# A fused macaron block on one core: the first packed chunk from SBUF to SBUF on two queues, and the expert weights fetched later

## The reference

```
x = x + 0.5 * ffn(layernorm(x))
x = x + dilated_attention(layernorm(x))
x = x + 0.5 * ffn(layernorm(x))

ffn(x):  x = conv3(x) + conv_b                   # 128 -> 128 channels, 3 taps
         q, k, v = split(x @ wqkv.T + bqkv)      # 16 heads of 8
         ctx = softmax(q k^T / sqrt(8)) v        # 512 x 512 for each head
         x = layernorm(x + ctx @ wo.T + bo) * g1 + b1
         probs = softmax(x @ gate_w + gate_b)    # 8 experts, all of them used
         y_e = relu(x @ w1[e] + b1[e]) @ w2[e] + b2[e]        # 128 -> 512 -> 128
         return layernorm(x + sum_e probs[e] * y_e) * g2 + b2
```

## Time and profile before

| | |
|---|---|
| median of 3 runs | 1558.36 us |
| profiled execution | 1559.22 us |
| its span, first to last instruction | 1557.5 us |
| mean granted PE clock | 0.982 |
| busy: PE, DVE, ACT, POOL | 96%, 75%, 72%, 65% |
| DMA, mean rate | 84 GB/s |

### The profile page before, as it was taken

The page is one execution under the profiler, slowest core; times in us unless marked ns, Lnnn a source line. Parts: engine busy times, 40 slices in busy tenths (PEclk is TensorE's granted clock), DMA queues, the critical chain, the costliest instruction groups (busy, mean ns, idle before and its releaser), DMA issues.

```text
span 1557.5 us, 26116 instructions
## 1 busy us (share of the span) xinstructions
PE 1502.6 (96%) x8318; PEld 832.5 (53%) x8318; DVE 1160.8 (75%) x1834; ACT 1121.3 (72%) x1636; POOL 1014.9 (65%) x978
## 2 busy tenths in 40 slices
PE   4888999999999999999999999999999999999997
PEld 3433555555555555555555555555555555555476
DVE  3767677878778787777877778777777777767486
ACT  2466777677776777777677777777777777777776
POOL 3521668767686776868767686776757677667343
PEclk7799999999999999999999999999999999999999
DMA  7433333152332514233142331514323251521111
GB/s 177 119 92 86 96 87 85 49 140 53 81 91 56 130 42 105 74 88 91 49 131 61 81 92 45 141 48 116 83 75 98 69 117 43 142 51 36 41 43 33
DMA packets 75309, 130.06 MB, mean 84 GB/s; under 512 B 10613, under 2 KB 39206, under 8 KB 70566
## 3 DMA queue, kind: packets, MB, share of 16 engines
q1 hardware_dynamic: 73894, 124.19, 31.2%
q0 software_dynamic: 1280, 4.20, 1.0%
HBM read 97.42 MB, written 29.62 MB: 82 GB/s over the span
## 4 chain that ended last, share of the span: by engine, by line
PE 84%; DVE 8%; issue 3%; SPq 1%; DMA 1%; ACT 1%; POOL 1%; DVEq 0%; ACTq 0%; POOLq 0%
PE hid_y L1013 16%; PE ctx_ps L1208 14%; PE hid_y L1017 13%; PE hid_y L1014 13%; PE score L1056 12%; DVE negmax L881 3%; PE misc L1013 2%; PE score L1076 1%; PE misc L1148 1%; DVE x1n L349 1%; PE score L1013 1%; PE misc L1105 1%; PE misc L1164 1%; PE misc L1141 1%; PE misc L1014 1%
## 5 line engine op out<-in xcount | busy, mean ns | idle before, releaser
L881 DVE TENSOR_REDUCE negmax<-score 128x2 f32<-128x1024 f32 x484 | 590.5, 1220 | 239.4 <-PE score L1056 239.4
L592 POOL TENSOR_TENSOR hidl<-hid,hidh 128x512 fp32r<-128x512 f32 x456 | 584.4, 1293 | 258.1 <-DVE hidh L838 140.8
L711 ACT ACTIVATE probs<-score 128x1024 f32<-128x1024 f32 x468 | 479.5, 1024 | 108.7 <-PE score L1076 108.5
L740 ACT ACTIVATE hid<-hid_y,cols 128x512 f32<-128x512 f32 x484 | 330.9, 684 | 161.9 <-PE hid_y L1017 154.2
L1208 PE MATMUL ctx_ps<-probs,V 128*18 128x512 f32 x2048 | 271.5, 602 | 3.2 <-DVE ctxT L888 3.2
L1056 PE MATMUL score<-Kp,Qp 24*128 24x512 f32 x968 | 244.9, 500 | 23.8 <-DMA Kp<-k_parts_dram 16.1
L1076 PE MATMUL score<-Qp,Kp 32*128 32x512 f32 (+1 forms) x1024 | 265.9, 499 | 0.0
L1013 PE MATMUL hid_y<-x1h,w1h 128*128 128x512 f32 x484 | 236.2, 488 | 1.5 <-DVE negmax L881 1.3
L369 POOL TENSOR_TENSOR yacc<-yacc,gated 128x512 f32<-128x512 f32 x127 | 170.6, 1343 | 61.8 <-DVE gated L854 61.8
L737 ACT ACTIVATE hidh<-hid_y,cols 128x512 fp32r<-128x512 f32 x256 | 174.7, 682 | 34.4 <-PE hid_y L1017 31.9
L1056 PEld LDWEIGHTS score<-Kp,Qp 24*128 24x128 f32 x968 | 90.5, 183 | 197.4 <-issue 138.2
(11 more groups left out here) (203 smaller groups left out, 1828.4 us busy)
## 6 DMA issues: line engine op xcount, KB each, us to landing
gate_b<-gate_dram SPq DMA_DIRECT2D x128, 256.0 KB, 3.6
q_parts_dram<-q_parts SPq DMA_DIRECT2D x48, 256.0 KB, 3.0
k_parts_dram<-k_parts SPq DMA_DIRECT2D x48, 256.0 KB, 3.1
Qp<-q_parts_dram SPq DMA_DIRECT2D x64, 192.0 KB
Kp<-k_parts_dram SPq DMA_DIRECT2D x64, 192.0 KB
Qp<-q_parts_dram SPq DMA_DIRECT2D x30, 240.0 KB
Kp<-k_parts_dram SPq DMA_DIRECT2D x30, 240.0 KB
Qp<-q_parts_dram SPq DMA_DIRECT2D x30, 144.0 KB
```

The lines of the kernel that those rows point to most:

```text
L592: pool.tensor_tensor(hidl[:, n % RING, :], hid[:, n % 2, :], hidh[:, n % RING, :].bitcast(F32), ALU.subtract).then_inc(s["h_lo"], 1)
L711: act.activation(probs[:, n % 2, 2 * j:2 * j + 2, :], score2[:], ACT.Exp, scale=SCALE)\
L740: act.activation(hid[:, n % 2, :], hid_bank(u, n), ACT.Relu, bias=col(n))\
L881: dve.tensor_reduce(negmax[:, g % 2, :, k % 8], banks_for_max(u.count(32, k))[:], AX.X, ALU.max, negate=True).then_inc(s["a_max"], 1)
```

## The change

Four things change, all in unit 0 and in the prelude of unit 1.

1. The first chunk of Qp and Kp for the maxima is written by `pack_first` straight from `parts`: 12 DMAs of 8 rows by 512 values for q on SP, and 12 for k on ACT. The three stores of k to DRAM move to ACT as well. All other chunks go through DRAM as before.
2. ACT issues the four m_rows DMAs of unit 0 (`MAX_BY_ACT = 1`); SP keeps those of all other units.
3. The splits of weight tiles 0 to 3 stay at ticks 0, 4, 8, 12; those of tiles 4 to 15 stand at ticks 28, 32, ..., 72, and their fetches 12 ticks ahead, at 16, 20, ..., 60.
4. `CLOCK_FILL` of round 14 is 10 instead of 12, the second f_xn load stands at tick -15 instead of -27, and unit 1's first k chunk is loaded at tick -11 instead of -16.

```
-CLOCK_FILL = {k: 12 if k == 14 else 1 if k % 2 == 0 else 0 for k in range(14, 56)}
-SECOND_LOAD_AT = -27
+SPLITS_FROM = 28
+CLOCK_FILL = {k: 10 if k == 14 else 1 if k % 2 == 0 else 0 for k in range(14, 56)}
+MAX_BY_ACT = 1
+SECOND_LOAD_AT = -15
...
-        SPLIT_EVERY = TICKS // (2 * E)
+        def by_act(n, k):
+            return n == 0 and k == 1
+
+        def packed(n, use, chunk):
+            first = 16 * HG * 2 * 3 if (use, chunk) == (0, 0) else CHUNK_LOADS
+            return first + (n - 1) * CHUNK_LOADS if n else 0
+
+        def pack_first(eng, k, part):
+            lo, hi = FIRST_CHUNKS[0][0]
+            for slot in RUNS[k][part]:
+                for half, at in enumerate(DATA_AT[0]):
+                    for pair in range(lo, hi):
+                        head = PAIRS * half + pair
+                        row = at + DH * slot
+                        eng.dma_start((Qp, Kp)[k][row:row + DH, pair, :].bitcast(F32),
+                                      parts[k][DH * head:DH * head + DH, part, :].bitcast(F32))\
+                            .then_inc(s["pack_in"][0][0], 16)
...
+        SPLIT_AT = [4 * k for k in range(GATE_RING)] + [SPLITS_FROM + 4 * k for k in range(2 * E - GATE_RING)]
+        FETCH_AT = {SPLIT_AT[k] - 12: k for k in range(GATE_RING, 2 * E)}
...
+        SECOND_LOADS_AT = {-19: (0, 0, 0), -11: (1, 0, 0), -7: (0, 1, 0), -6: (1, 1, 0),
+                           1: (0, 0, 1), 2: (1, 0, 1), 25: (0, 1, 1), 26: (1, 1, 1)}
...
                 for k, at in ((0, u.at["f_qs"]), (1, u.at["f_ks"])):      # sync
-                    if T == at:
+                    if T == at and not by_act(u.n, k):
...
+                        if u.n == 0:
+                            for part, written in enumerate(("f_p1", "f_p2")):
+                                wait_sp(s[written], 1)
+                                pack_first(sp, 0, part)
...
-                if T - 1 in NM_AT:
+                if T - 1 in NM_AT and u.n >= MAX_BY_ACT:
...
-                if i0 == 0 and T == t and t % SPLIT_EVERY == 0:           # gpsimd, scalar
-                    k = t // SPLIT_EVERY
+                if u.n == 0 and T in SPLIT_AT:
+                    k = SPLIT_AT.index(T)
-                if i0 == 0 and T == t and t % SPLIT_EVERY == 1 and t // SPLIT_EVERY + GATE_RING < 2 * E:
-                    load_expert(t // SPLIT_EVERY + GATE_RING)
+                if u.n == 0 and T in FETCH_AT:
+                    load_expert(FETCH_AT[T])
...
+                        if by_act(u.n, k):                                # scalar, behind k's f_p1
+                            for part, written in enumerate(("f_p1", "f_p2")):
+                                wait(act, s[written], 2)
+                                pack_first(act, 1, part)
+                            for part in range(2):
+                                for run in RUNS[k][part]:
+                                    act.dma_start(dram[k][run].rearrange("d h q -> h d q"),
+                                                  parts[k][:, part, :].bitcast(F32)).then_inc(s["parts_out"][k], 16)
...
+                    if u.n < MAX_BY_ACT:                                  # scalar, behind m_rows
+                        wait(act, s["a_mr"], u.count(4, g + 1))
+                        act.dma_start(Qp[MAX_ROW:MAX_ROW + MAX_ROWS, 2 * g:2 * g + 2, :].bitcast(F32), m_rows[:])\
+                            .then_inc(s["a_m_in"], 16)
```

More of the change, by code:

```diff
@@ L381, in qk_bank, with load_packed @@
             return misc[:] if n else score2[:, k, :]
-        SPLIT_EVERY = TICKS // (2 * E)
+        def by_act(n, k):
[13 more added lines that the diff above has]
+                            .then_inc(s["pack_in"][0][0], 16)
+        def load_packed(eng, n, k, use, chunk):
+            lo, hi = chunks_of(n)[use][chunk]
+            for half, at in enumerate(DATA_AT[use]):
+                eng.dma_start((Qp, Kp)[k][at:at + PRODUCT_ROWS, lo:hi, :].bitcast(F32).rearrange("p i q -> p (i q)"),
+                              dram[k][:, :, PAIRS * half + lo:PAIRS * half + hi, :]
+                              .rearrange("a d i q -> (a d) (i q)")).then_inc(s["pack_in"][use][chunk], 16)
+        SPLIT_AT = [4 * k for k in range(GATE_RING)] + [SPLITS_FROM + 4 * k for k in range(2 * E - GATE_RING)]
+        FETCH_AT = {SPLIT_AT[k] - 12: k for k in range(GATE_RING, 2 * E)}
         FIRST_LOADS_AT = {-19: (0, 0, 0), -16: (1, 0, 0), -7: (0, 0, 1), -6: (1, 0, 1),
                           1: (0, 1, 0), 2: (1, 1, 0), 25: (0, 1, 1), 26: (1, 1, 1)}
+        SECOND_LOADS_AT = {-19: (0, 0, 0), -11: (1, 0, 0), -7: (0, 1, 0), -6: (1, 1, 0),
+                           1: (0, 0, 1), 2: (1, 0, 1), 25: (0, 1, 1), 26: (1, 1, 1)}
         LOADS_AT = {-19: (0, 0, 0), -16: (1, 0, 0), -7: (0, 1, 0), -6: (1, 1, 0),
@@ L445, in tick @@
                 for k, at in ((0, u.at["f_qs"]), (1, u.at["f_ks"])):
-                    if T == at:
-                        for use in s["pack_in"]:
-                            for chunk_in in use:
-                                wait_sp(chunk_in, u.count(CHUNK_LOADS, 0))
+                    if T == at and not by_act(u.n, k):
+                        for use in range(2):
+                            for chunk in range(2):
+                                wait_sp(s["pack_in"][use][chunk], packed(u.n, use, chunk))
+                        if u.n == 0:
+                            for part, written in enumerate(("f_p1", "f_p2")):
+                                wait_sp(s[written], 1)
+                                pack_first(sp, 0, part)
                         for part, written in enumerate(("f_p1", "f_p2")):
@@ L454, in tick @@
                                              parts[k][:, part, :].bitcast(F32)).then_inc(s["parts_out"][k], 16)
[L455 to L464, removed]
-                if T - 1 in NM_AT:
+                loads = (FIRST_LOADS_AT, SECOND_LOADS_AT)[u.n] if u.n < 2 else LOADS_AT
+                if T in loads:
+                    k, use, chunk = loads[T]
+                    if u.n or (use, chunk) != (0, 0):
+                        wait_sp(s["parts_out"][k], u.count(48, 48))
+                        wait_sp(s[("a_s1", "a_s2")[use]], (u.n - 1) * 32 + TC * chunks_of(u.n)[use][chunk][1])
+                        load_packed(sp, u.n, k, use, chunk)
+                if T - 1 in NM_AT and u.n >= MAX_BY_ACT:
                     g = NM_AT[T - 1]
@@ L646, in tick @@
             def tick(T, u, t, i, i0):
-                if i0 == 0 and T == t and t % SPLIT_EVERY == 0:
-                    k = t // SPLIT_EVERY
+                if u.n == 0 and T in SPLIT_AT:
+                    k = SPLIT_AT.index(T)
                     src, loaded, value = staged(k)
@@ L1034, in pack_ready @@
             def pack_ready(use, n, pair):
-                for chunk_in, (first_pair, _) in zip(s["pack_in"][use], chunks_of(n)[use]):
+                for chunk, (first_pair, _) in enumerate(chunks_of(n)[use]):
                     if pair == first_pair:
-                        wait(pe, chunk_in, (n + 1) * CHUNK_LOADS)
+                        wait(pe, s["pack_in"][use][chunk], packed(n + 1, use, chunk))
             def ready_for_max(n, k):
```

## The result

The changed kernel takes 1572.37 us (median of 4 runs, 1570.55 to 1578.44) against 1557.98 for the kernel before on the same chip: ratio 1.0092, 95% interval 1.0075 to 1.0109, so 14.4 us slower. The forecast was 14.2 us faster, 1544.2 us, and the range ended at 1552.5. The profiled execution took 1572.75 us (span 1570.6, mean clock 0.973 instead of 0.982).

The account below looks back on a forecast made before the run. PE, busy 96% of the span, was taken as the bound, with savings only in the first 110 us. Terms -8.2 - 1.3 - 0.7 - 4.8 + 0.8 = -14.2 us gave 1544.2 us; range 1538.5 to 1552.5.

Parts of the forecast that it names:

- Step 1: First chunk of unit 0: small direct copies at 0.32 us pitch start round 0 at 25.0 instead of 34.69, gain 9.7.
- Rival A: First chunk: the small copies are slow, at 59 GB/s, round 0 at 28 to 31, about 1549 us; chance 0.17.
- Step 2: Rounds 8 and 12: later chunks through DRAM give back 1.5 of 9.7 us; round 12 comes 8.2 earlier, at 41.2.
- The worst end: Lower bound of the whole sum: 3.5 + 0.7 - 2.0 = 2.2 us of gain, giving 1556.2 us.
- Step 2's maxima: Round 12: m_rows of group 0, issued by ACT at about 37.5, takes 3.7 us to land, at 41.2.
- step 4: Round 28: group 2's maxima on ACT's queue land in 3.5 to 4 us; with the clock, gain 4.8, bounds 0 and 6.9.
- Step 3: Rounds 12 to 14: f_xn ready earlier on POOL, gain 1.3 us; two fills fewer, 0.7; round 14 at 48.2.
- Step 5: Costs: ACT's m_rows issues ahead of exps, 0.8 us (0 to 2.0); splits, K load and f_xn load 0.
- The k load at 0: Unit 1's K load at tick -11 instead of -16 passes no other issue in SP's stream: cost 0.
- cover for step 2: Second chunk: expert weights no longer fetched in this stretch, which lets the undisturbed transfer rate be used, taken as 155 GB/s.

Follow-up runs that it names:

- last experiment: Kernel before with late weights, unit 1's first k load at tick -11, second f_xn load at -15, 10 fills; chunk and maxima as before: 1552.54 us, ratio 0.9962.

## Why the prediction was wrong

| | before | predicted | measured |
|---|---|---|---|
| round 0 | 34.69 | 25.0 | 28.86 |
| round 8 | 43.68 | 35.0 | 44.23 |
| round 12 | 49.39 | 41.2 | 56.80 |
| round 14 | 58.36 | 48.2 | 63.77 |
| wait at round 28 | 4.83 | 1.5 | 4.34 |
| clock after 109 us | full | full | half to 133 |
| span against before | | -14.2 | +13.1 |

- **Step 1**, the first chunk: the term that failed is the issue of a copy, 0.32 us taken from an 8-row load of another kind, 0.85 measured. The upper bound (0.95 from the fill, round 0 at 31.2) held it; the choice between far ends went to the wrong row. The fill was the nearer one: SBUF to SBUF, a few partitions, on the same queue. Rival A had the right size of the delay with the wrong reason, a rate of the engines; these were idle for three quarters of the time.
- **Step 2**, what is late next, failed even in its bounds. I let the second chunk follow at its own rate, but its stores and loads stand behind the copies: Q's load is issued at 34.52, 5.6 us later than before, and round 8 waits 5.72. In a bound with copies at 0.95 us this delay belonged too, and then no gain was left. The worst end of 2.2 us of gain was not a worst end.
- **Step 2's maxima and step 4** failed in the mechanism. I put 3.7 us for a transfer that "stands behind nothing"; it took 10.7 at round 12, and round 28 still waited 4.34. With the maxima gone from SP nothing held back the loads of ticks 25 and 26, another 0.79 MB behind the 0.79 MB that I had counted (pairs 0 to 3); no term of the sum had them. Of the two rules weighed there, the Trainium skill (DMA: Bandwidth & Descriptors, Queues, rings and completion order) has the engine take turns between queue rows; by it the landing would have been near 3 us, an estimate, and the 10.7 do not bear it out: none of the 36 packets got a turn for 7 us. In the kernel before with the maxima on ACT they did go beside SP's last loads, from 47.7 us on, so the rule is not refuted in general. The same page's Rules for kernel authors, that a second issuing engine brings no bandwidth and saves issue time only, agrees with both findings: 10.6 instead of 18.6 us of issue, and maxima that land with the loads.
- **Step 3**, f_xn and the fills: right here, no wait for f_xn, 10 fills in 3.55 us, and the clock is up from the next round on (0.50 at 65.65), as before. The 0.7 us for two fills fewer isn't shown as a gain: the last experiment has them fewer and gains nothing by it.
- **Step 5**, costs: 0.8 us for three ACT issues. The one at 106.46 delays the split behind it by 0.71 us, as costed; what I did not have is that the clock falls 3 us later and stays down for 24 us, 7.6 us lost. The splits cost nothing, as said. The k load at 0 was wrong for the kernel before (4.4 us of gain by itself) and right only since step 4 had emptied its place.
- **The late weights**, which I had as cover for step 2 and no term of their own, are the best part: 7.2 us alone. The gain at round 0 is one and the same for them and the direct chunk, and they get it without 24 issues.

The sum by runs: the rest of the change -5.9 us (last experiment); the direct chunk on top of it +5.0 (0.9994 against 0.9962); the maxima on ACT on top of both +15.3 (1.0092 against 0.9994), of which about 6 to 8 are the clock and most of the rest the loads ahead of group 0. Together +14.4. The ratios come from different chips, and each step is uncertain by 3 to 4 us, so the 5.0 of the chunk is only just clear of noise; by itself, in one comparison, it cost 4.8 (1.0031, 1.0020 to 1.0043).

Two of these costs have their mechanism shown. Not settled is what makes the clock fall at 109 us. PE had at most 0.06 us without work in the 5 us before, and in the kernel before with the maxima on ACT, with the same issue of group 3, eight of ten runs have a mean clock of 0.980 or more. Late waits upstream, ACT's issue and the fetches beside it come together in the changed kernel; only the issue was tried by itself. The wait at round 12 isn't needed for it, since the kernel with the loads held falls too.

## What to carry to other kernels

A wait on an in-order queue is also a gate for what stands behind it: before moving it to another queue, list what will then start early and what that meets. Many small copies are paid by the issue, not by their bytes, so take the price from the nearest row of the same kind, and carry it through to everything queued behind. When a transfer is late, look first for other transfers that can go later; this cost nothing and gave what the direct way was meant to give.

## What the runs showed of the hardware

- A copy of 8 rows by 512 values from SBUF to SBUF held its issuing queue for 0.67 us with nothing beside it (engines busy for 14%), and for 0.84 to 0.95 us in the first twelve on a queue (engines busy for 26% in the changed kernel).
- A 16 KB transfer on ACT's queue let PE go on 10.7 us after its issue, with 1.00 MB of SP's earlier loads and 0.70 MB of weights moved meanwhile (161 GB/s), and 4.5 us after it on SP's queue with the loads behind it. For the first 7 us not one of its 36 packets was moved.
- A read of the packed chunk let PE start 3.0 to 3.1 us after its issue without weight fetches beside it, and 6.7 us after it with them.
- PE ran at half clock (1.2 GHz) from 109 to 133 us while its windows show it busy all the time; a second kernel had the same for 24 us, from 105 to 129. A lower mean clock shows in single runs of other kernels too: 0.006 lower and 6 us more in two of ten runs with the maxima on SP, 0.013 lower and 14 us more in one run of the kernel before.
